# One core, graph layers, experts and gated recurrence: normalization behind the experts on ScalarE, the next chunk's splits moved up, column sums in groups

## What is computed

```python
x = x + _L0_ffn_ref(_layernorm(x, axis=-1)[None], ...)[0]
x = x + _L1_gnn_ref(_layernorm(x, axis=-1), edge_index, edge_weight, ...)   # five steps
x = x + _L1_ffn_ref(_layernorm(x, axis=-1)[None], ...)[0]

h = x                                              # inside _L1_gnn_ref
for i in range(weight.shape[0]):
    m = h @ weight[i]
    msgs = m[src] * edge_attr[:, None]
    agg = jax.ops.segment_sum(msgs, dst, num_segments=n_nodes)
    h = gru_cell(agg, h, w_ih, w_hh, b_ih, b_hh)

logits = jnp.mean(x, axis=1) @ Wr + br             # inside _L1_ffn_ref: one mean over all tokens
```

## Time and profile before

| | us |
|---|---|
| median of 3 runs (lowest, highest) | 3867.06 (3864.45, 3872.6) |
| profiled execution: its own time | 3872.27 |
| its span, first to last instruction | 3870.7 |
| TensorE busy (share, instructions) | 3051.9 (79%, 18100) |
| VectorE busy | 2375.8 (61%, 5044) |
| ScalarE busy | 1530.7 (40%, 3100) |
| mean granted TensorE clock | 0.937 |

### The profile page before, as it was taken

How to read it: one execution, slowest core, us unless ns; L and a number is a source line. 1 busy time by engine, 2 the same in 40 slices (tenths; PEclk the granted TensorE clock), 3 DMA queues, 4 the chain that set the end, 5 groups by cost and what they waited for, 6 DMA issues and landing times.

```text
span 3870.7 us, 54544 instructions
## 1 busy us (share of the span) xinstructions
PE 3051.9 (79%) x18100; PEld 2747.6 (71%) x18101; DVE 2375.8 (61%) x5044; ACT 1530.7 (40%) x3100; POOL 1414.4 (37%) x921
## 2 busy tenths in 40 slices
PE   2455454201999994999949999999999999999798
PEld 2444453101888883888849988998998899899677
DVE  7999996511787876555575555455545555555447
ACT  2344342110444552333334444444444444444255
POOL 1577888788877774878800000000000000000000
PEclk9999998655999996999979999999999999999889
DMA  9877335684667655535263333343433343344000
GB/s 395 265 226 196 38 48 118 188 255 79 177 166 204 181 129 172 136 86 136 33 225 125 129 119 128 119 131 117 134 127 119 127 129 122 126 132 131 37 31 29
DMA packets 378074, 538.46 MB, mean 139 GB/s; under 512 B 125779, under 2 KB 283642, under 8 KB 374458
## 3 DMA queue, kind: packets, MB, share of 16 engines
q1 hardware_dynamic: 251076, 487.82, 37.1%
q0 software_dynamic: 119088, 19.33, 8.8%
q10 hardware_dynamic: 7750, 29.17, 2.1%
HBM read 398.99 MB, written 137.25 MB: 139 GB/s over the span
## 4 chain that ended last, share of the span: by engine, by line
PE 44%; DVE 4%; DMA 1%; ACT 1%; issue 0%; SPq 0%; POOL 0%; ACTq 0%; DVEq 0%
PE bank L607 43%; DVE ring_lo L1702 1%; PE bank L786 1%; PE bank L855 1%; DMA yg_end<-chosen 0%; DVE gates_sb L1728 0%; ACT ring_hi L1107 0%; DVE gates_sb L1727 0%; DVE res_b L1814 0%; DVE xT L1729 0%; DVE v_lo L1759 0%; DVE stats L1780 0%; DVE stats L1817 0%; DVE nat L1789 0%; DMA past_res<-chosen 0%
## 5 line engine op out<-in xcount | busy, mean ns | idle before, releaser
L506 POOL DMA_INDIRECT plane_w<-pair,slot x392 | 658.0, 1679 | 188.4 <-issue 128.4
L500 POOL DMA_INDIRECT plane_a<-pair,slot x392 | 624.1, 1592 | 267.6 <-issue 123.4
L607 PE MATMUL bank<-ring_hi,h_hi 128*128 128x448 f32 x1750 | 652.7, 373 | 60.9 <-DVE ring_lo L1702 55.5
L1702 DVE TENSOR_TENSOR ring_lo<-ring_lo,ring_hi 128x448 fp32r<-128x448 f32 x875 | 522.8, 621 | 220.4 <-ACT ring_hi L1107 219.9
L1107 ACT ACTIVATE ring_hi<-ring_lo 128x448 fp32r<-128x448 f32 x875 | 497.3, 576 | 384.6 <-PE bank L607 378.0
L607 PE MATMUL bank<-ring_lo,h_hi 128*128 128x448 f32 x1750 | 643.5, 368 | 0.0
L607 PE MATMUL bank<-ring_hi,h_lo 128*128 128x448 f32 x1750 | 643.1, 367 | 0.0
L554 POOL DMA_DIRECT2D v_lo<-gru_v x5 | 3.6, 722 | 1388.1 <-PE bank L607 1311.9
L607 PE MATMUL bank<-gring_hi,hs_hi 128*128 128x512 f32 (+2 forms) x700 | 261.6, 374 | 256.6 <-DVE gring_lo L1417 256.6
L607 PEld LDWEIGHTS bank<-ring_hi,h_hi 128*128 128x128 f32 x1750 | 331.1, 189 | 89.8 <-DVE h_lo L1769 49.3
L1720 DVE SCALAR_TENSOR_TENSOR gates_sb<-bank,bhh,gates_sb 128x448 f32<-128x448 f32 x70 | 47.9, 685 | 516.7 <-ACT gates_sb L1131 516.7
(11 more groups left out here) (349 smaller groups left out, 6742.2 us busy)
## 6 DMA issues: line engine op xcount, KB each, us to landing
ring_lo<-plane_w SPq DMA_DIRECT2D x175, 1120.0 KB, 5.5
gring_lo<-plane_a SPq DMA_DIRECT2D x50, 1280.0 KB
plane_a<-nat SPq DMA_DIRECT2D x25, 1600.0 KB, 43.4
plane_w<-nat SPq DMA_DIRECT2D x100, 400.0 KB
w_hl<-w_split SPq DMA_DIRECT2D x16, 2048.0 KB
part_in<-in_L_ffn_W SPq DMA_DIRECT2D x16, 1024.0 KB
w_split<-part_hi SPq DMA_DIRECT2D x16, 1024.0 KB
w_split<-part_lo SPq DMA_DIRECT2D x16, 1024.0 KB
```

What stands on the lines that cost most here:

```text
L500: g_.indirect_dma_start(out=plane, out_offset=bass.IndirectOffsetOnAxis(slot[:, t:t + 1], 0), in_=pair[:, k, t:t + 1], in_offset=None, com ...
L506: g_.indirect_dma_start(out=plane_w, out_offset=bass.IndirectOffsetOnAxis(slot[:, n:n + 1], 0), in_=pair[:, 0, n:n + 1], in_offset=None, c ...
L607: last = mm(ps, lhs[x], rhs[y], start=start and n == 0, stop=stop and n == 2)
L1702: V.tensor_tensor(ring_lo[:, t, :], ring_lo[:, t, :].bitcast(FP32), ring_hi[:, t % HS, :].bitcast(FP32), ALU.subtract).then_inc(lo_rdy, 1)
```

## The change

1. Behind the experts, VectorE no longer normalizes. It writes -mean * rstd over `mean` with one small operation a group (`off_ready`), and ScalarE normalizes the group's five tiles into `nat` with an activation that has scale and bias, each counted in `nat_ready`, then goes on as before. What waited for `RR` = 5 counts of `nat_ready` (SyncE ahead of the `whh` load, GpSimd ahead of `v_lo`) waits for 25, and TensorE for single tiles.
2. SyncE issues panel r of chunk 0 behind `load_chosen(5r + 3)`. Before, panel 0 was issued ahead of the wait for the experts' last scatters and panel r + 1 behind the fifth load of group r.
3. The first five high and low parts of chunk 1 come ahead of `split_h(0, 0)`, `whh` and `v`, on ScalarE and on VectorE.
4. Behind the recurrence VectorE goes in four groups of 8, 8, 6 and 3 tiles (`TOKEN_GROUPS`): adds, the inverse root of the group before, statistics, moments. ScalarE normalizes all tiles. TensorE sums tiles 0 to 7 between `turn_back(19)` and `turn_back(20)`, then 8 to 15 and 22 to 24; tiles 16 to 21 are summed over the tiles by VectorE into `fo`, and TensorE adds that one tile.

```diff
@@ -56,6 +56,7 @@
 TE = 7
 TURNS = {**{t: [t - 4] for t in range(4, 4 + TE)}, **{t: [2 * t - 29, 2 * t - 28] for t in range(18, NT)}}
 RR = NT // RB
+TOKEN_GROUPS = (0, 8, 16, 22, NT)
 X0, H0 = 8, 1024
 WW = KD * H0 + H0 // 128 * D
 PW = WW // 2
...
@@ -423,18 +424,17 @@
 
             sp.wait_ge(y_rdy, ST + 1)
             sp.wait_ge(scat_w, 16 * ET)
-            load_panel_w(0, 0, 0)
             for b in range(2):
                 sp.wait_ge(y_out[b], 16 * ((ST + 1 - b) // 2))
             for r in range(RR):
                 for t in range(r * RB, (r + 1) * RB):
                     load_chosen(t)
-                if r + 1 < RR:
-                    load_panel_w(0, 0, r + 1)
+                    if t % RB == 3:
+                        load_panel_w(0, 0, r)
             sp.wait_ge(moe_done, 1)
             sp.dma_start(res_d, res[:, :, :].rearrange("p t f -> p (t f)")).then_inc(res_kept, 16)
             sp.wait_ge(res_kept, 16)
-            sp.wait_ge(nat_ready, RR)
+            sp.wait_ge(nat_ready, NT)
             sp.dma_start(whh, a["L1_gnn_w_hhT"].rearrange("(k p) g -> p k g", p=128)).then_inc(gru_in, 16)
             sp.dma_start(bih[:, :], a["L1_gnn_b_ihT"]).then_inc(gru_in, 16)
             sp.dma_start(bhh[:, :], a["L1_gnn_b_hhT"]).then_inc(gru_in, 16)
...
@@ -545,7 +545,7 @@
             scatter_result(ST - 1)
 
             pool.wait_ge(res_kept, 16)
-            pool.wait_ge(nat_ready, RR)
+            pool.wait_ge(nat_ready, NT)
             for b in range(2):
                 pool.wait_ge(v_kept[b], 16 * ((LAYERS + 1 - b) // 2))
             with pool.Fori(0, LAYERS) as i:
...
@@ -836,24 +836,36 @@
                 pe.wait_ge(back_lo, t + 1)
                 pe.wait_ge(lo_rdy, t + 1)
                 sums_of(t, 0)
-                pe.wait_ge(nat_ready, 1 + t // RB)
+                pe.wait_ge(nat_ready, t + 1)
                 turn_nat(t)
             for q in range(1, GC * LAYERS):
                 i, c = divmod(q, GC)
                 aggregate_w(i, c, back=c == 0, turn=c == GC - 1 and i < LAYERS - 1)
             for j in range(KD):
                 gate_products(GC * LAYERS - 1, j)
-            for t in range(NT):
-                turn_back(LAYERS, t)
-
-
-            pe.wait_ge(back_lo, NT * (LAYERS + 1))
-            for t in range(NT):
+            def add_to_mean(t, first=False):
                 pe.wait_ge(nat_t, t + 1)
                 rows = 128 if t < NT - 1 else LAST
                 for k in range(KD):
-                    last = mm(bank[k][:, 0:1], nat_b[0:rows, t, k * 128:(k + 1) * 128], ones[0:rows, 0:1], start=(t == 0), stop=(t == NT - 1))
+                    mm(gate_ps[k][:, 0:1], nat_b[0:rows, t, k * 128:(k + 1) * 128], ones[0:rows, 0:1], start=first, stop=False)
+
+            for t in range(TOKEN_GROUPS[2] + 4):
+                turn_back(LAYERS, t)
+            for t in range(TOKEN_GROUPS[1]):
+                add_to_mean(t, t == 0)
+            for t in range(TOKEN_GROUPS[2] + 4, NT):
+                turn_back(LAYERS, t)
+            for t in range(TOKEN_GROUPS[1], TOKEN_GROUPS[2]):
+                add_to_mean(t)
+            for t in range(TOKEN_GROUPS[3], NT):
+                add_to_mean(t)
+            pe.wait_ge(f_part, 1)
+            for k in range(KD):
+                last = mm(gate_ps[k][:, 0:1], fo[:, 0, k * 128:(k + 1) * 128], ones[:, 0:1], start=False, stop=True)
             last.then_inc(f_mean, 1)
+
+
+            pe.wait_ge(back_lo, NT * (LAYERS + 1))
             pe.wait_ge(f_meanT, 1)
             pe.wait_ge(f_in, 64)
             for k in range(KD):
...
@@ -1172,8 +1184,11 @@
             for g in range(RR):
                 at = slice(g * RB, (g + 1) * RB)
                 root(std[:, at], var[:, at])
-                act.wait_ge(nat_ready, 1 + g)
+                act.wait_ge(off_ready, 1 + g)
                 for t in range(g * RB, (g + 1) * RB):
+                    A(nat[:, t, :], res[:, t, :], ACT.Identity, bias=mean[:, t:t + 1], scale=rstd[:, t:t + 1]).then_inc(nat_ready, 1)
+                for t in range(g * RB, (g + 1) * RB):
+                    act.wait_ge(nat_ready, t + 1)
                     A(h_hi[:, t, :], nat[:, t, :], ACT.Copy).then_inc(back_hi, 1)
                     high(0, t)
                 if g > 0:
...
@@ -1181,12 +1196,12 @@
                         take_nat(t)
             for t in range(NT - RB, NT):
                 take_nat(t)
+            for t in range(HS):
+                high(1, t)
             split_h(0, 0, 0)
             act.wait_ge(gru_in, 48)
             A(whh_hi[:, :, :], whh, ACT.Copy).then_inc(whh_h, 1)
             round_v(0)
-            for t in range(HS):
-                high(1, t)
             for q in range(1, GC * LAYERS):
                 i, c = divmod(q, GC)
                 chunk_w(i, c, first=c == 0, turn=c == GC - 1 and i < LAYERS - 1, more=q < GC * LAYERS - 1)
...
@@ -1196,11 +1211,12 @@
             for j in range(KD):
                 gates_n(GC * LAYERS - 1, j)
 
-            root(std[:, :], var[:, :])
-            act.wait_ge(rstd_b, 1)
-            for t in range(1, NT, 2):
-                act.wait_ge(nat_t, t)
-                A(nat_b[:, t, :], res_b[:, t, :], ACT.Identity, bias=noff[:, t:t + 1], scale=rstd[:, t:t + 1]).then_inc(nat_t, 1)
+            for g in range(len(TOKEN_GROUPS) - 1):
+                lo, hi = TOKEN_GROUPS[g], TOKEN_GROUPS[g + 1]
+                root(std[:, lo:hi], var[:, lo:hi])
+                act.wait_ge(rstd_b, g + 1)
+                for t in range(lo, hi):
+                    A(nat_b[:, t, :], res_b[:, t, :], ACT.Identity, bias=noff[:, t:t + 1], scale=rstd[:, t:t + 1]).then_inc(nat_t, 1)
 
             def split_x(c, width):
                 act.wait_ge(tr_out, 2 * NT + c * CT + width // 128)
...
@@ -1785,11 +1801,10 @@
                 v.wait_ge(std_ready, roots[0] + 1)
                 roots[0] += 1
                 link(V.reciprocal(rstd[:, at], std[:, at]))
-                for t in range(g * RB, (g + 1) * RB):
-                    last = V.tensor_scalar(nat[:, t, :], res[:, t, :], mean[:, t:t + 1], rstd[:, t:t + 1], ALU.subtract, ALU.mult)
-                link(last)
-                v.sem_inc(nat_ready, 1)
+                V.scalar_tensor_tensor(mean[:, at], mean[:, at], -1.0, rstd[:, at], ALU.mult, ALU.mult).then_inc(off_ready, 1)
             split_group(RR - 1)
+            for t in range(HS):
+                low(1, t)
             split_h(0, 0)
             v.wait_ge(whh_h, 1)
             V.tensor_tensor(whh_lo[:, :, :], whh, whh_hi[:, :, :].bitcast(FP32), ALU.subtract).then_inc(whh_set, 1)
...
@@ -1797,8 +1812,6 @@
             v.wait_ge(g_dve, 1)
             v.wait_ge(whh_set, 1)
             rest_of_v(0)
-            for t in range(HS):
-                low(1, t)
             v.wait_ge(tr_out, 2 * NT)
             for q in range(1, GC * LAYERS):
                 i, c = divmod(q, GC)
...
@@ -1809,25 +1822,34 @@
             new_h(GC * LAYERS - 1, GC - 1)
 
             v.wait_ge(res_back, 16)
-            for t in range(NT):
-                v.wait_ge(back_ps, NT * (LAYERS - 1) + t + 1)
-                V.tensor_tensor(res_b[:, t, :], res_b[:, t, :], turned_tile(LAYERS, t), ALU.add).then_inc(back_lo, 1)
-            v.wait_ge(back_lo, NT * (LAYERS + 1))
-            for t in range(NT):
-                last = V.bn_stats(stats[:, t, :], res_b[:, t, :])
-            link(last)
-            moments(NT).then_inc(var_ready, 1)
-            inverse_root()
-            link(V.scalar_tensor_tensor(noff[:, :], mean[:, :], -1.0, rstd[:, :], ALU.mult, ALU.mult))
-            v.sem_inc(rstd_b, 1)
-            for t in range(0, NT, 2):
-                if t > 0:
-                    v.wait_ge(nat_t, t)
-                V.tensor_scalar(nat_b[:, t, :], res_b[:, t, :], mean[:, t:t + 1], rstd[:, t:t + 1], ALU.subtract, ALU.mult).then_inc(nat_t, 1)
+
+            def inverse_group(g):
+                at = slice(TOKEN_GROUPS[g], TOKEN_GROUPS[g + 1])
+                v.wait_ge(std_ready, roots[0] + 1)
+                roots[0] += 1
+                link(V.reciprocal(rstd[:, at], std[:, at]))
+                V.scalar_tensor_tensor(noff[:, at], mean[:, at], -1.0, rstd[:, at], ALU.mult, ALU.mult).then_inc(rstd_b, 1)
+
+            for g in range(len(TOKEN_GROUPS) - 1):
+                lo, hi = TOKEN_GROUPS[g], TOKEN_GROUPS[g + 1]
+                for t in range(lo, hi):
+                    v.wait_ge(back_ps, NT * (LAYERS - 1) + t + 1)
+                    V.tensor_tensor(res_b[:, t, :], res_b[:, t, :], turned_tile(LAYERS, t), ALU.add).then_inc(back_lo, 1)
+                if g > 0:
+                    inverse_group(g - 1)
+                v.wait_ge(back_lo, NT * LAYERS + hi)
+                for t in range(lo, hi):
+                    last = V.bn_stats(stats[:, t, :], res_b[:, t, :])
+                link(last)
+                moments(hi - lo, lo).then_inc(var_ready, 1)
+            inverse_group(len(TOKEN_GROUPS) - 2)
+            v.wait_ge(nat_t, TOKEN_GROUPS[3])
```

(4 more changed lines are left out.)

4 lines of the change are left out of this document (2 added, 2 removed).

## The result

The changed kernel takes **3852.37 us** (median of 6 runs, 3850.46 to 3857.88) where the kernel before takes 3866.84 (6 runs, 3864.45 to 3872.6) beside it: ratio 0.9957, 95% interval 0.9947 to 0.9968. That is 14.5 us less by the medians; 16.9 were forecast (3850.2, range 3843 to 3858). The profiled execution took 3850.46 us with a span of 3848.8; the profiled one of before had been a long one of its kind.

The account below looks back on a forecast made before the run. TensorE's recurrent product, left alone, dominates; behind the experts VectorE was taken as the first bound. Terms -7.1 + 0 - 0.4 - 9.4 = -16.9 us gave 3855.4 for the profiled execution, 3850.2 for the median, range 3843 to 3858.

Parts of the forecast that it names:

- the side that had 0.92: Whole kernel: faster by more than about 0.2%, under 3859.3 us, given 0.92.
- A: Stretch behind the experts, 1944 to 2039 us: VectorE bounds it first; terms -7.1, 0 and -0.4 us.
- B: Last normalization and column sums, 3646 to 3688 us: working in token groups across the engines gives -9.4 us.
- A2: Panel loads behind the experts: +0.5 us at tile 4, -0.5 in later groups, together 0; ends +2.5 and -0.8.
- A1: Normalization behind the experts moved to ScalarE: VectorE saves 1.78 us in each of groups 0 to 3, -7.1 us.
- A3: Chunk 1's first splits ahead of the weights': gates start 2.4 us earlier but at a slow clock, net -0.4 us.
- R1: Rival, column sums: they run at the high clock, -12.8 us there, 3846.8 us in all; chance 0.12.
- R2: Rival, behind the experts: panels and loads still collide, that stretch gains 0, 3857.3 us; chance 0.09.
- R3: Rival, behind the experts: panel landings of 14.9 us delay loads by 28.1 us in all, 3878.3 us; chance 0.01.
- R4: Rival, behind the experts: TensorE at half clock bounds the stretch, about 10 us more, 3860 us; chance 0.03.

Follow-up runs that it names:

- front_early: Changed kernel with panel 0's load moved back ahead of the wait for the last expert outputs; ratio 0.9946 to the kernel before.
- reduce_undone: Changed kernel without VectorE's strided reduce, TensorE summing those six tiles too; 34.69 us from the first add to the means, against 31.95.
- b_alone: Kernel before with only the change's last normalization (token groups, ScalarE normalizing, new sums); ratio 0.9977 to the kernel before.
- before_again: Kernel before, unchanged, traced once more; 495 first-layer matmuls in 100 us, against 485 in its first trace.

## Why the prediction was right, and where it was not

**Right in the time, and in part by luck**: 3852.37 lies 2.2 us above the forecast, in the range, and on the side that had 0.92. By the stretches the change is worth 3.3 us in the lead, 3.5 in A and 9.8 in B (41.50, 41.55 and 41.66 against 31.95, 31.73, 31.73 and 31.74 for traces with B as changed), 16.6 together; the sum was 16.9. The part behind the experts gave 6.8 of its 7.5. The luck is in A2, whose two misses cancel.

- **A1, the freed VectorE (-7.1)**: held. A group went from 13.74-14.35 to 11.9-12.5 us (groups 1 to 4), and ScalarE's Identities took 0.51 each. From group 0's statistics to group 4's are 51.6 us in before's form (mean of three) and 44.8 in after's (six): 6.8 less. The last group gave nothing, as said: from its statistics to tile 24's eviction it is 19.8 to 19.9 us in before's form and in four traces of after's, 20.9 and 21.1 in the other two.
- **A2, the loads (0)**: the sum held, and the account of it did not. It let panel 0 move ahead of tile 4's load for +0.5 and took 0.5 back in later groups; measured are +2.8 (11.63 against 8.87, the means of six and three traces), above its own end of 2.5. The rate was right in kind (1.15 MB at 328 GB/s are 3.5 us); what I did wrong was to set that load's new landing by when the queue would be empty and to take the near end. A load issued behind 1.15 MB waits for most of its transfer: 6.91 less 4.15 is 2.8 of 3.5 us. And it took panel 0 to have cost nothing under the wait for the scatters. It had cost 3.3 us there: the last scatter lands in 5.74 to 5.88 us beside the panel and in 2.41 or 2.42 without it. front_early, which moves the panel alone, shows both.
- **A3, the splits (-0.4)**: a small miss. From tile 24's eviction the gates start 1.5 us earlier than in before's form (2.4 forecast), and their slow clock takes 1.9 on the mean of five, 0.1 to 2.8 in single traces (2.0 forecast): +0.4. The new pause is 4.67 us long (about 5 forecast), but 3.1 in two of the five. Panel 0 of chunk 1 did not "just hold": it was 0.9 us late here and up to 1.8 in other traces. It stands behind the `whh` load, which waits for the last normalization, and landed 18.6 us after the split began (17.1 forecast).
- **B (-9.4)**: -9.55 in this trace, with its parts: 0.87 a tile, wait 3.37, normalizations 0.51. The strided sum, which has no row ahead, took 2.77 us and not 2.1: 1.80 ns a value, 1.77 over 2048 values, against 1.35 in the earlier trace rows. By the Trainium skill (SBUF — State Buffer, "Door 1: The DMA port swizzle", the note on 16-byte cachelines) such a read pays for each line; the traces agree in sign, a third more. That the stride is the cause is not shown, since the row differs in more: 456 neighbouring values on one partition. The sum was hidden, which reduce_undone shows from the other side.
- **Rivals.** R1 (sums at the high clock) did not come in the changed kernel, but did for most of the first eight tiles in b_alone's trace; the other sums stayed at 0.50. The rule of the Trainium skill named there (TensorE: Matmul & The Clock Gate, "What's actually happening") would have all of them at the high level; reduce_undone's 14.75 us of sums without a gap stayed at half. R2, that loads and panels collide, came true for panel 0 alone, at either of its places. R3 and R4 did not show: the panels of chunk 0 landed in 5.5 to 7.9 us in the changed kernel's trace, and of TensorE's products in the last two groups only tile 15's and the begin of tile 16's ran at half the clock.

## What to carry over

When a large load stands beside or in front of a small transfer that an engine waits for, charge the small one with nearly the large one's whole transfer time, bytes over the rate seen (here 2.8 and 3.3 us of 3.5). That goes for the place that the load leaves as well as for the one it gets: a load that lies under a wait is not free if it makes the wait longer. An operation moved up on one engine only moves the place where the next one waits, so follow the chain to the first instruction that needs all of it (here the gate products, which stood behind a normalization, two weight loads and four splits; shortening that chain gave 8 us against front_early, and putting it in another order nothing that shows). And compare stretches between two landmarks in several traces, since the whole time of a long kernel hides 3 us that the stretch shows at once. Begin the stretch ahead of everything that the edit can touch: read from the first combine load alone, this change shows half of what it does, and front_early a gain that is not there.

## What the runs showed of the hardware

- **A large load delays a small transfer beside it.** A panel of 1.15 MB issued within 0.2 us of the last scatter of expert outputs brings that scatter's landing from 2.41-2.42 us (six traces) to 5.74-5.88 (eight). Issued by SyncE in front of a combine load of 0.26 MB it makes that load land late: VectorE's statistics behind it begin at 11.63 us (mean of six) and not at 8.87 (mean of three).
- **A pace that the granted clock does not show.** One unchanged kernel ran its first layer's matmuls 206.7 ns apart in one execution and 202.4 in another, from about 2045 to 2270 us, at a granted clock of 1.00 both times. Behind that it is mostly 202.4 in all, with shorter slow spells (before_again has one from about 2275 to 2305). Six of the fourteen traces have the slow pace from 2045 on, and Rec is 4.7 us longer in them. That is as large as most single edits here. What draws it is not known.
- **TensorE's clock after a pause.** The same 36 to 37 gate matmuls took 7.5 to 7.7 us in the four traces without a pause in front; 10.1 to 10.4 behind a pause of 4.7 us (three traces); 7.8, 9.2 and 9.2 behind 3.1 to 3.2; and 7.6, 7.7, 7.8 and 9.2 behind 1.9. In these traces the fall came more often behind the longer pauses, and at one length it could go either way.
- **One-column sums.** They stay at 0.50 though TensorE is recorded busy without a gap for 14.75 us; in one trace of eleven it stood at 0.97 for 2 us, from 0.8 us behind their begin, with transposes right in front of them as in the others.
- **A strided fp32 reduce.** 1.8 ns a value at 1536 and at 2048 values a partition, with 1 KB between neighbours.
